# Raw transposed x into the query product, the scale across tokens behind it, and a later low pass of f_out

## What is computed

```python
def _layernorm(x, axis=-1, eps=1e-05):
    m = jnp.mean(x, axis=axis, keepdims=True)
    v = jnp.var(x, axis=axis, keepdims=True)
    return (x - m) / jnp.sqrt(v + eps)
...
q = (x @ Wq + bq).reshape(B, N, NUM_HEADS, HEAD_DIM)      # L0: 16 heads of 16
attn = jax.nn.softmax(jnp.einsum('bnhd,bmhd->bhnm', q, k) * scale, axis=-1)
out = jnp.einsum('bhnm,bmhd->bnhd', attn, v).reshape(B, N, IMAGE_DIM)
h = jax.nn.relu(out @ W1 + b1)
return h @ W2 + b2
...
x = x + _L0_xattn_ref(_layernorm(x, axis=-1), ctx_768, ...)
x = x + _L0_ffn_ref(_layernorm(x, axis=-1), ...)     # top 2 of 8 LoRA experts around one 256-1024-256 net
x = x + _L1_xattn_ref(_layernorm(x, axis=-1), ctx_768, ctx_768, ...)   # one head over 64 keys
x = x + _L1_ffn_ref(_layernorm(x, axis=-1), L1_ffn_weight, L1_ffn_disha)
```

## Time and profile before

| | us |
|---|---|
| median of 3 runs | 335.01 |
| lowest, highest | 334.4, 338.75 |
| the profiled execution | 334.57 |
| its span, first to last instruction | 332.4 |
| PE busy in it | 316.3 (95%) |
| mean granted TensorE clock | 0.994 |

### The profile page before, as it was taken

The page is one execution under the profiler, slowest core; times in us unless marked ns, Lnnn a source line. Parts: engine busy times, 40 slices in busy tenths (PEclk is TensorE's granted clock), DMA queues, the critical chain, the costliest instruction groups (busy, mean ns, idle before and its releaser), DMA issues.

```text
span 332.4 us, 6489 instructions
## 1 busy us (share of the span) xinstructions
PE 316.3 (95%) x2507; PEld 288.4 (87%) x2507; DVE 234.0 (70%) x644; ACT 173.4 (52%) x355; POOL 145.7 (44%) x149
## 2 busy tenths in 40 slices
PE   8779998999999999999999999999999999999992
PEld 6567997799998999899979997999889988999771
DVE  3965378565779567866876787767786669456766
ACT  3336836673575646572676267534755554534411
POOL 1924481635135631735072806280546234613341
PEclk9999999999999999999999999999999999999997
DMA  7679540003100130004100310023001200000000
GB/s 255 170 204 365 145 105 2 2 2 87 41 0 3 40 89 32 2 16 109 40 0 2 95 65 0 2 72 89 2 0 42 55 35 1 2 0 34 0 34 32
DMA packets 14366, 18.85 MB, mean 57 GB/s; under 512 B 2144, under 2 KB 10720, under 8 KB 14080
## 3 DMA queue, kind: packets, MB, share of 16 engines
q1 hardware_dynamic: 12464, 15.12, 16.4%
q10 hardware_dynamic: 1872, 3.31, 2.9%
HBM read 9.51 MB, written 2.62 MB: 37 GB/s over the span
## 4 chain that ended last, share of the span: by engine, by line
PE 83%; DVE 6%; ACT 3%; POOL 3%; DMA 2%; issue 1%; SPq 1%; DVEq 0%; ACTq 0%
PE psI L290 13%; PE psI L446 13%; PE psI L299 11%; PE psP L299 10%; PE psS L299 6%; PE psT L290 4%; PE psP L381 3%; PE psS L367 2%; PE psP L382 2%; PE psT L314 2%; PE psT L513 2%; PE psS L344 2%; POOL hid_l L1428 2%; PE psI L608 1%; PE psP L600 1%; DVE kb L1380 1%
## 5 line engine op out<-in xcount | busy, mean ns | idle before, releaser
L1409 POOL TENSOR_TENSOR rs<-ve,mhalf 128x2 f32<-128x2 f32 x30 | 22.5, 750 | 99.0 <-DVE ve L1034 99.0
L1428 POOL TENSOR_TENSOR hid_l<-r,hid_h 128x512 fp32r<-128x512 f32 x32 | 40.9, 1293 | 15.3 <-ACT hid_h L836 15.3
L1113 DVE SCALAR_TENSOR_TENSOR r<-psI,nbi,r 128x256 f32<-128x256 f32 x60 | 25.8, 479 | 25.3 <-PE psI L446 25.3
L446 PE MATMUL psI<-at_h,lb_h 128*128 128x256 f32 x120 | 36.5, 305 | 2.0 <-DVE at_l L1105 1.5
L1422 POOL TENSOR_TENSOR hs_l<-hs,hs_h 128x512 fp32r<-128x512 f32 x16 | 20.7, 1293 | 38.6 <-ACT hs_h L816 38.5
L1054 DVE RECIPROCAL rec<-psP 128x256 f32<-128x256 f32 x16 | 28.0, 1752 | 8.5 <-PE psP L382 8.5
L446 PE MATMUL psI<-at_l,lb_h 128*128 128x256 f32 x120 | 33.9, 282 | 0.0
L446 PE MATMUL psI<-at_h,lb_l 128*128 128x256 f32 x120 | 33.8, 282 | 0.0
L831 ACT ACTIVATE r<-psI,first 128x256 f32<-128x256 f32 x60 | 24.2, 469 | 13.6 <-PE psI L446 13.5
L446 PEld LDWEIGHTS psI<-at_h,lb_h 128*128 128x128 f32 x120 | 22.6, 188 | 8.6 <-issue 5.0
L800 ACT ACTIVATE ex<-psS 128x512 f32<-128x512 f32 x32 | 19.0, 596 | 20.7 <-PE psS L367 20.6
(11 more groups left out here) (258 smaller groups left out, 870.9 us busy)
## 6 DMA issues: line engine op xcount, KB each, us to landing
stack<-qu_h SPq DMA_DIRECT2D x60, 64.0 KB, 2.0
xin<-in_x SPq DMA_DIRECT2D x8, 256.0 KB, 2.8
stack<-qu_l SPq DMA_DIRECT2D x32, 64.0 KB, 2.0
out<-x ACTq DMA_DIRECT2D x7, 256.0 KB, 2.0
raw_wi<-in_wi SPq DMA_DIRECT2D x1, 1024.0 KB, 7.2
raw_wo<-in_wo SPq DMA_DIRECT2D x1, 1024.0 KB, 10.9
kv<-in_kv SPq DMA_DIRECT2D x2, 384.0 KB, 9.8
raw_w<-in_w ACTq DMA_DIRECT2D x1, 512.0 KB, 6.8
```

What stands on the lines that cost most here:

```text
L446: last = mm(bank[:, k * T:(k + 1) * T], (WH, WL)[x]["lb"][:, 0, f * P:(f + 1) * P], AT[y][:, which, :], start=False, stop=q == 2, skip_gro ...
L1113: last = V.scalar_tensor_tensor(out=R1[:, f, :], in0=bank[:, k * T:(k + 1) * T], scalar=nbi[:, f:f + 1], in1=R1[:, f, :], op0=MAX, op1=ADD)
L1409: G_.tensor_tensor(rs[:, :], ve[:, :], mhalf[:, :], ALU.pow).then_inc(S(f"ln{j}_rs"), 1)
L1428: G_.tensor_tensor(HL[:, two, :], R1[:, two, :], as32(HH[:, two, :]), ALU.subtract).then_inc(S("hidl"), 1)
```

## The change

From block 1 on x is no longer normalised and transposed on the chip for the queries. The host hands over x once more, transposed (`xt`); `load_xt` brings it into xn1; ACT's `across_high` and a POOL subtraction split it into XTA. `Wq` has its column means taken off in the start: PE's `query_means` and one DVE subtraction, before the split into high and low, for all blocks (block 0 keeps its normalising). The factor rs of each token must lie along the free axis behind the product: SP's `across` writes rs (128x2) to DRAM and reads it back to all partitions as `scales`; DVE's `queries_scaled` multiplies the product by it into Q32, in SBUF; ACT's `queries` and DVE's `queries_low` read that.

In body, f_out(f, 0)'s low pass goes behind f_out(f, 1)'s two high passes. In body(0) ten fillers stand in place of 3 + 5 around the transposes. `across(1)` and the transfers of block 1 lie in SP's queue as shown. Some semaphores are merged, with the same waits or later ones.

```diff
@@ -146,11 +146,15 @@
     YB = [YS[:, :, at:at + D] for at in LINEAR]
     gb = sb("gb", [P, BATCH * KEYS])
+    scales = sb("scales", [P, T])
+    qs = sb("qs", [P, KC * T])
 
     xin, xr, xmid, xg, xn1 = (sb(n, [P, NT * D]) for n in ("xin", "xr", "xmid", "xg", "xn1"))
     XIN, XMID, XG = r3(xin, NT), r3(xmid, NT), r3(xg, NT)
     XN = {j: r3(t, NT) for j, t in ((1, xn1), (2, xn2))}
     XTA = pair("xta", KC, KC * T)
+    XT, Q32 = r3(xn1, KC), r3(qs, KC)
+    SCALES = scales[:, :].rearrange("p (n t) -> p t n", t=NT)
     QU = pair("qu", KC, KC * T)
@@ -199,6 +203,7 @@
     CTX, CTXD, WK1, WV1 = 2 * D, 2 * D, 0, 2 * D
 
+    dr_scales = nc.dram_tensor("dr_scales", (T,), F32, kind="Internal").ap()
     dr_kd = [nc.dram_tensor(n, (P, BATCH * KC * P), F32, kind="Internal").ap() for n in ("dr_kdh", "dr_kdl")]
@@ -219,9 +224,27 @@
             def load_x(b):
                 if b > 0:
-                    sp.wait_ge(S("ln1_xh"), b * NT)
+                    if b == 1:
+                        sp.wait_ge(S("ln1_xh"), NT)
+                    sp.wait_ge(S("ln1_st"), b * NT)
                     sp.wait_ge(S("xres"), b)
                 sp.dma_start(XIN, x_v[b]).then_inc(S("x_in"), 16)
+
+            def load_xt(b):
+                if b == 1:
+                    sp.wait_ge(S("ln1_T"), 1)
+                else:
+                    sp.wait_ge(S("ln1_l"), b)
+                sp.dma_start(xn1[:, :], io["xt"][b * P:(b + 1) * P, :]).then_inc(S("xt_in"), 16)
+
+            def across(b):
+
+                sp.wait_ge(S("ln1_rs"), b + 1)
+                if b > 1:
+                    sp.wait_ge(S("q32"), (b - 1) * KC)
+                sp.dma_start(dr_scales.rearrange("(p t) -> p t", p=P), lnst[1][4][:, :]).then_inc(S("scales_out"), 16)
+                sp.wait_ge(S("scales_out"), b * 16)
+                sp.dma_start(scales[:, :], dr_scales.unsqueeze(0).broadcast_to([P, T])).then_inc(S("scales_in"), 16)
 
@@ -257,18 +280,21 @@
             keys_in(1, 2)
             stack_q(0, 1)
+            load_xt(1)
             load("w2")
             load("ga")
             load("wi")
             load("lb")
             load("wo")
             sp.dma_start(late[:, :], io["late"]).then_inc(S("ld_late"), 16)
-            sp.dma_start(kv1[:, :], io["kv1"]).then_inc(S("ld_kv1"), 16)
+            sp.dma_start(kv1[:, :], io["kv1"]).then_inc(S("ld_passing"), 16)
             sp.dma_start(passing[:, :], io["passing"]).then_inc(S("ld_passing"), 16)
             sp.dma_start(GWR[:, :, KEYS:KEYS + D], io["wc"].rearrange("p (c n) -> p c n", c=KC)).then_inc(S("ld_wc"), 16)
             for b in range(1, NBLK):
                 if b > 1:
                     load_x(b)
+                    load_xt(b)
+                across(b)
                 stack_q(b, 0)
...
@@ -541,6 +567,15 @@
 
 
+            def query_means():
+
+                pe.wait_ge(S("consts"), 1)
+                pe.wait_ge(S("ld_wq"), 16)
+                for c in range(KC):
+                    last = mm(I_(1)[:, 0:D], avg[:, 0:1].broadcast_to([P, P]), raw["wq"][:, c * D:(c + 1) * D],
+                              start=c == 0, stop=c == KC - 1)
+                last.then_inc(S("wq_mean"), 1)
+
             def keys0():
...
@@ -685,17 +720,9 @@
                     f_first(f, 3)
                 if a == 0:
-                    filler(I_(0), 3)
-                    transposes(1, h, T_(1))
-                    filler(I_(0), 5)
+                    filler(I_(0), 10)
                 if A_:
                     a_hidden(a, 0)
-                if H_ and a > 0:
-                    if f == 0:
-                        pe.wait_ge(S("gw"), 1)
-                    if C_:
-                        pe.wait_ge(S("z"), (c + 1) * NT)
-                    transposes(1, h, T_(1))
                 if A_:
@@ -711,16 +738,21 @@
                     a_out(a, 1)
                 if F_:
-                    f_out(f, 0)
+                    f_out(f, 0, low=False)
                 if H_:
                     a_row_scores(h, 1)
                 if F_:
                     f_out(f, 1, low=False)
+                    f_out(f, 0, high=False)
                 if a == 0:
                     constant_row()
                     keys1()
                     values1()
                 if A_:
+                    if f == 0:
+                        pe.wait_ge(S("gw"), 1)
+                    if C_:
+                        pe.wait_ge(S("z"), (c + 1) * NT)
                     transposes(2, a, T_(1))
@@ -744,10 +776,11 @@
 
 
-            pe.wait_ge(S("zeros"), 1)
+            pe.wait_ge(S("consts"), 3)
             filler(P_(1), 4)
             keys0()
-            filler(P_(1), 3)
+            query_means()
+            filler(P_(1), 2)
             pe.wait_ge(S("ld_first"), 16)
@@ -782,11 +815,21 @@
                 A(dst[0], bank.rearrange("p (c n) -> p c n", c=KC), ACT.Identity).then_inc(S(f"ln{j}_h"), 1)
 
+            def across_high(b):
+
+                act.wait_ge(S("xt_in"), b * 16)
+                act.wait_ge(S("q_ps"), b)
+                A(XTA[0], XT, ACT.Identity).then_inc(S("ln1_h"), 1)
+
             def queries(b):
-                act.wait_ge(S("q_ps"), b + 1)
                 for m in range(KC):
-                    A(QU[0][:, m, :], P_(0)[:, m * T:(m + 1) * T], ACT.Identity,
-                      bias=cols[:, BQ + m:BQ + m + 1]).then_inc(S("qh"), 1)
+                    if b == 0:
+                        act.wait_ge(S("q_ps"), 1)
+                        src = P_(0)[:, m * T:(m + 1) * T]
+                    else:
+                        act.wait_ge(S("q32"), (b - 1) * KC + m + 1)
+                        src = Q32[:, m, :]
+                    A(QU[0][:, m, :], src, ACT.Identity, bias=cols[:, BQ + m:BQ + m + 1]).then_inc(S("qh"), 1)
 
@@ -860,7 +903,10 @@
 
             def high_weights(n):
-                act.wait_ge(S("ld_" + n), 16)
+                if n == "wq":
+                    act.wait_ge(S("wq_in"), 1)
+                else:
+                    act.wait_ge(S("ld_" + n), 16)
                 A(wh[n][:, :], raw[n][:, :], ACT.Identity).then_inc(S("hi_w"), 1)
@@ -926,7 +972,7 @@
                     high_weights("w2")
                 if H_:
-                    normalise(1, h, XIN)
+                    across_high(h)
                 if F_:
@@ -941,10 +987,7 @@
                     A(gw_h[:, :], gw[:, :], ACT.Identity).then_inc(S("gw_h"), 1)
                 if a == 0:
-                    high(1, h, XTA, T_(1))
                     high_weights("wi")
-                if H_ and a > 0:
-                    high(1, h, XTA, T_(1))
                 if A_:
@@ -988,12 +1031,12 @@
             load("wq")
             load("w1")
-            high_weights("wq")
             act.wait_ge(S("kt0_ps"), 1)
             act.wait_ge(S("ld_first"), 16)
             for m in range(KC):
                 A(kt0_h[:, m * P:(m + 1) * P], I_(0)[:, m * P:(m + 1) * P], ACT.Identity,
                   bias=cols[:, BK0 + m:BK0 + m + 1]).then_inc(S("kt0_h"), 1)
+            high_weights("wq")
             normalise(1, 0, XIN)
@@ -1038,10 +1081,18 @@
                     S(f"ln{j}_l"), 1)
 
+            def queries_scaled(b):
+                dve.wait_ge(S("q_ps"), b + 1)
+                dve.wait_ge(S("scales_in"), b * 16)
+                for m in range(KC):
+                    V.tensor_tensor(Q32[:, m, :].rearrange("p (t n) -> p t n", t=NT),
+                                    P_(0)[:, m * T:(m + 1) * T].rearrange("p (t n) -> p t n", t=NT), SCALES,
+                                    MULT).then_inc(S("q32"), 1)
+
             def queries_low(b):
                 dve.wait_ge(S("qh"), (b + 1) * KC)
                 for m in range(KC):
-                    V.scalar_tensor_tensor(out=QU[1][:, m, :], in0=P_(0)[:, m * T:(m + 1) * T],
+                    V.scalar_tensor_tensor(out=QU[1][:, m, :], in0=P_(0)[:, m * T:(m + 1) * T] if b == 0 else Q32[:, m, :],
                                            scalar=cols[:, BQ + m:BQ + m + 1], in1=as32(QU[0][:, m, :]),
@@ -1284,13 +1335,13 @@
                     dve.wait_ge(S("x3"), (c + 1) * NT)
                     norm_stats(4, c, X3)
-                if H_:
-                    low(1, h, XTA, T_(1))
                 if f == 0:
                     dve.wait_ge(S("gw_h"), 1)
                     V.tensor_tensor(gw_l[:, :], gw[:, :], as32(gw_h[:, :]), SUB).then_inc(S("gw_l"), 1)
                 if a == 0:
                     low_weights("wi", 1, 2)
+                if H_:
+                    queries_scaled(h)
                 if F_:
@@ -1357,25 +1408,28 @@
                 V.tensor_tensor(r3(kt1, KC), I_(0)[:, 0:KC * P].rearrange("p (m n) -> p m n", m=KC),
                                 cols[:, BK1:BK1 + KC].unsqueeze(2).broadcast_to([P, KC, P]), ADD).then_inc(S("kt1"), 1)
-                dve.wait_ge(S("ld_passing"), 16)
+                dve.wait_ge(S("ld_passing"), 32)
                 dve.wait_ge(S("v1_ps"), 1)
```

(30 more changed lines are left out.)

4 lines of the change are left out of this document (2 added, 2 removed).

## The result

| | before | after |
|---|---|---|
| median, us | 334.81 (4 runs) | 345.51 (4 runs) |
| lowest, highest | 334.4, 338.75 | 344.25, 346.01 |
| span of the profiled execution | 332.4 | 344.0 |

The account below looks back on a forecast made before the run. PE, 95% busy, was taken to bound the kernel, with a dependent chain at the start. 334.57 + 6.4 (start and queue) + 1.0 (clock) - 2.4 (bodies) = 339.6 us, range 336.0 to 343.0.

Parts of the forecast that it names:

- the start: DVE's chain to kd_l and stack_q: centring and wq_l's split make SP reach the bulk loads 1.7 us later.
- the broadcast: Read-back of block 1's scales to all partitions: 128 KB, taken at 2.1 us like the 64 KB transfers' 2.0.
- the clock: PE idle from about 40 to 45 lets the granted clock fall: +1.0 us, bounds 0 and 2.05.
- the bodies: Bodies 1 to 7: -2.4 us together, as 0.8 in body 1, 0.25 each in 2 to 6, 0.3 in 7.
- Landing in order: SP's queue: loads land in issue order, load_xt(1) adds 0.75, the scales' write lands 0.4 behind wc, at 41.45.
- Rival 1: SP's queue: the small scales transfer is not held up, scales there by 35; 334.6 us, change even; chance 0.10.
- The centring's 0.95: Start, DVE: centring Wq waits for query_means and takes 0.69, so kt0_l begins 0.95 us late.
- wq_l's 0.69: Start, DVE: low_weights("wq"), formerly in idle time, stands behind kd_h in the chain and adds 0.69 us.
- Rival 2: Scales' write and read-back each take their own time after the queue empties, 6.8 instead of 2.5; 343.9 us; chance 0.14.
- f_out's move: Bodies: moving the low pass of t=0 later removes the wait for hid_l, 0.35 us a body, 0.25 taken in 2 to 6.
- The four transposes' 0.44: PE, bodies 1 to 6: removing transposes(1, h) frees 0.44 us, kept only in body 1.
- the added latency: Middle bodies: queries_scaled on DVE makes hs_l begin 0.5 us later; PE waits 0.37 at the pass.

Follow-up runs that it names:

- experiment 2: The changed kernel with POOL's ks operation waiting until DVE has done kd_l; 343.32 us, ratio 1.0253 to the kernel before.
- experiments 1: The changed kernel with block 1's scales written between the loads of w2 and ga and read back between wi and lb; 338.24 us, ratio 1.0102.
- 9: The kernel before with f_out's low pass of t=0 moved later and ACT's hidden_high(a, 1) ahead of queries(h); 331.98 us, ratio 0.9914.
- experiment 8: The changed kernel with the broadcast reading 128 different rows of xt instead of one row 128 times; 341.85 us, without an interval.
- experiment 5: The changed kernel with 15 more filler units (30 matmuls) on PE ahead of block 1's first row scores; 344.97 us, without an interval.
- experiment 12: The changed kernel with blocks 0 and 1 on normalised x, ks behind kd_l, hidden_high ahead of queries and 15 filler units; 329.47 us, ratio 0.9857.
- experiment 7: The kernel before with f_out's low pass of t=0 moved later and POOL's ks behind kd_l; 333.48 us, ratio 0.9974.
- experiment 11: The kernel before with f_out's low pass moved, ks behind kd_l, and 15 filler units for 8 ahead of block 0's first scores; 331.8 us, ratio 0.9915.

## Why the prediction was wrong, step by step

It forecast 339.6 us, same; measured were 345.51, slower, outside the range. The mechanism that it put first is the one that happened: block 1's scales land behind the bulk loads, and PE waits. What failed are four terms of its sum, all too small on the same side: the start (+1.7, measured +2.7), the broadcast (2.1, measured 4.8), the clock (+1.0, measured +1.3) and the bodies (-2.4, measured about 0).

- *Landing in order* (right). wc took 12.4 for a forecast 11.7 + 0.75, and the 1 KB landed 0.4 behind it, as put. Rival 1 is out.
- *The start, +1.7* (mis-sized: +2.7 at wc's issue, 29.56 for 26.87). The centring's 0.95 was of the right kind: kt_l stood 0.66 us further behind kt_h than before. It did not show, because PE's product of the keys ended at 6.21, where the prediction had 6.98 from the one execution of before; that is luck. wq_l's 0.69 was right. What was missing is the collision of DVE with POOL, 1.7 us between these two executions; experiment 2 takes it away. It could be seen in the trace of before: kb took 4.08 there for 1.21. The step took the durations of one execution as fixed, where a shift of the queue changes which operation is caught. The Trainium skill (SBUF — State Buffer, "SBUF: two separate sides") says that DVE and GpSimd take turns at a shared port pair where the DVE operation has two inputs in SBUF and the GpSimd one reads SBUF, and that the one that starts second waits for the whole of the other. The traces agree, but for the length of a turn. In all eight traces in which ks ran beside these operations, the caught one ended as if it had begun 3.5 us behind ks' start and run undisturbed: before, kb from 13.41, with ks at 9.90; after, the second kd_h from 12.58, with ks at 9.04. Where DVE's kb had begun first (experiments 1 and 9), ks took 6.37 and 6.31 for 5.37 and the turn came that much later. In the last 1.9 us of ks nothing was held: wq_l ran in 0.68 at 12.88. Why ks holds the others for 3.5 of its 5.37 us, or whether the end that the profile gives it is late, isn't shown.
- *The broadcast, 2.1* (mis-sized by 2.7: it took 4.8, a median of 4.3). The nearest row was taken to be the 64 KB transfers between SBUF places, 2.0. That row has 64 KB of different data. Here one row of DRAM is read 128 times, and with another source it is 1.7 less (experiment 8). Rival 2's deciding point, scales at 45.7, was passed (they came at 47.1), but only half of its mechanism happened: the write landed 0.4 behind wc, and neither 3.2 nor 2, and the read was longer than the 3.6 that the rival gave it.
- Together: the write landed 0.9 later (42.35 for 41.45) and the broadcast took 2.7 longer, so the scales came 3.5 later than 43.6, and the row scores 3.6 later, at 48.61 for 45.0. Experiment 1 shows by taking the wait away that this is what the time hangs on.
- *The clock, +1.0*: 1.3 (experiment 5), within its bounds; with the 0.2 of waiting for hs_l the stretch behind the row scores lost 1.5.
- *The bodies, -2.4* (mis-sized: about 0; +0.2 in body 1, 0.0 in bodies 2 to 6, -0.3 at the end). f_out's move gave 0.36, about as put. The four transposes' 0.44 was to be cancelled by the added latency; it was outweighed. hs_l was to begin 0.5 later and began 0.55 later (2.02 for 1.47 behind the product): right. But hs_l also takes 0.26 longer, because queries_low now reads the scaled product from SBUF beside it. That put the pass 0.72 later behind the product, for a forecast 0.37, and the 0.35 between them cancels f_out's 0.36 in bodies 2 to 6. In body 1 qu_l stood beside hid_l (3.00 us for 0.87), and the forecast gain of 0.8 became a loss of 0.2.
- The sum of the misses is 3.6 + 0.5 + 2.4 = 6.5; the spans of the profiled executions give 11.6 - 5.0 = 6.6, with 5.0 the forecast change.

The prediction's range was too narrow because each bound stood alone. The upper end of the broadcast's bound (+1.5), the clock's upper bound (+1.05) and the bodies' lower gain (+1.6) add up to 343.8, and that still lacks the collisions, for which it had no term.

## What to carry to other kernels

A transfer that a compute engine waits for must not stand behind the bulk loads of the start; if it can't be issued ahead of them, the step that needs it should begin with a later block (experiment 12: with block 1 left out of the change, two edits of order and seven more units of filler, 1.0287 became 0.9857). When an operation is put between a product and the engine that reads it, look at what that engine does next for others, and let it do that first: it was the difference between 0.36 us lost and 0.36 gained in every body. When an operand moves from PSUM to SBUF or a DVE queue is shifted, look for the POOL operation beside it.

## What the runs showed of the hardware that was not expected

- One row of 1 KB, just written, read 128 times from DRAM into 128 partitions took a median of 4.3 us, 128 different rows of the same size 2.6 (experiment 8).
- A write of 1 KB to DRAM among bulk loads went with landings of 6.5 to 7.9 instead of 3.8 us (w2) and 8.6 to 11.3 instead of 7.3 (wi), in the three runs where it stood between them, with single packets of 8 KB taking up to 4.2 us for 0.31.
- A shorter start can give its time back to the clock: one made shorter by 2.2 us gave 0.7 at the next mark (experiment 7), since PE stood idle for 1.8 and then worked at 0.57 of the clock; the way to the mark took 16.5 us there and 15.1 with the clock at 1.00 (experiment 11).
- DVE operations with two SBUF inputs beside a POOL operation: the kd_h pair 4.73 us for 0.75, kb 4.08 for 1.21, qu_l 3.08 for 0.87; and the POOL side, hs_l, 1.56 for 1.29. POOL's ks held them off for its first 3.5 us, in eight traces.
